# Six of 31 expert blocks added by one-hot products on TensorE, and a weight sum cut into twelve pieces inside the block loop

## The reference, cut to what matters

```
xn = layernorm(x)                                  # layer 1, feed-forward
idx = top_k(xn @ router.T + router_bias, 2)        # 2 of 16 experts a token, no capacity limit
for e in range(16):
    h = silu(xn @ Wu[e]) * (xn @ Wg[e])            # 256 -> 128
    out += combine[:, e:e+1] * (h @ Wd[e])         # 128 -> 256
x = x + tanh(g) * (out + shared_expert(xn))
...                                                # layer 2, attention
gamma_w = clip(mean(abs(w)), 1e-5, None)           # layer 2, feed-forward: for each of 3 weights
w_dq = clip(round(w / gamma_w), -1, 1) * gamma_w   # 256 x 1024 each, ternary
```

## Time and profile before

| what | value |
|---|---|
| median of 3 runs | 891.05 us |
| the profiled execution | 892.17 us |
| its span, first to last instruction | 890.4 us |
| PE, DVE, ACT, POOL busy | 714.0, 534.0, 368.7, 303.3 us |
| mean granted TensorE clock | 0.889 of full speed |
| layer 1's block loop | about 477 to 531 us from the span's start |
| from its end to layer 2's first projection | about 531 to 563 us |

### The profile page before, as it was taken

The page is one execution under the profiler, slowest core; times in us unless marked ns, Lnnn a source line. Parts: engine busy times, 40 slices in busy tenths (PEclk is TensorE's granted clock), DMA queues, the critical chain, the costliest instruction groups (busy, mean ns, idle before and its releaser), DMA issues.

```text
span 890.4 us, 14503 instructions
## 1 busy us (share of the span) xinstructions
PE 714.0 (80%) x5356; PEld 501.8 (56%) x5356; DVE 534.0 (60%) x1244; ACT 368.7 (41%) x658; POOL 303.3 (34%) x332
## 2 busy tenths in 40 slices
PE   5987798997588788887889980892966579999997
PEld 3445465676355555555657860471444446777776
DVE  3896855667899999996475545827776530000014
ACT  4002022424799999996222323342663122221210
POOL 2941130000277777775007506300320072000024
PEclk9997899997899999897898995796898569999999
DMA  7311174520199999999204848000013132515413
GB/s 239 132 59 48 26 148 159 197 74 1 23 176 193 161 198 169 183 174 161 102 25 118 146 126 279 10 0 1 0 54 137 47 87 91 207 48 182 160 39 118
DMA packets 139133, 100.08 MB, mean 112 GB/s; under 512 B 109204, under 2 KB 125238, under 8 KB 137016
## 3 DMA queue, kind: packets, MB, share of 16 engines
q1 hardware_dynamic: 132552, 81.19, 37.8%
q0 software_dynamic: 6224, 17.96, 7.6%
q10 hardware_dynamic: 288, 0.00, 0.0%
HBM read 61.15 MB, written 10.72 MB: 81 GB/s over the span
## 4 chain that ended last, share of the span: by engine, by line
PE 34%; issue 11%; DVE 10%; POOL 4%; ACT 4%; DMA 3%; POOLq 0%; DVEq 0%; ACTq 0%
PE psum L2342 7%; PE psum L2361 5%; PE psum L1661 3%; PE psum L1938 2%; PE psum L214 2%; ACT both L1332 2%; POOL both L568 2%; PE psum L1676 1%; DVE xnT L1438 1%; PE psum L1242 1%; PE psum L2372 1%; PE psum L1520 1%; DMA both<-both 1%; PE psum L621 1%; PE psum L635 1%
## 5 line engine op out<-in xcount | busy, mean ns | idle before, releaser
L1153 POOL TENSOR_SCALAR both<-both 128x1024 f16<-128x1024 f32 x128 | 133.7, 1045 | 162.8 <-ACT both L1332 155.0
L1438 DVE TENSOR_SCALAR_CACHE_REDUCE xnT<-psum,both 128x1024 bf16<-128x1024 f32 x128 | 157.5, 1278 | 9.1 <-PE psum L1242 8.9
L1332 ACT ACTIVATE both<-psum,both 128x1024 f32<-128x1024 f32 x128 | 153.5, 1210 | 9.2 <-DVE xnT L1438 8.7
L1242 PE MATMUL psum<-both 128*128 128x512 bf16 x256 | 84.4, 415 | 32.2 <-ACT both L1332 28.0
L2342 PE MATMUL psum<-both 128*128 128x320 f32 x256 | 73.5, 441 | 3.8 <-ACT both L556 3.8
L1263 PEld LDWEIGHTS psum<-both 128*128 128x128 f16 x1024 | 63.3, 98 | 22.7 <-DMA both<-both 8.3
L2421 ACT ACTIVATE both<-psum 128x320 f32<-128x320 f32 x64 | 27.6, 437 | 110.0 <-PE psum L2342 92.1
L1263 PE MATMUL psum<-both 128*128 128x16 f16 x1024 | 67.7, 171 | 6.4 <-DMA both<-both 2.8
L1264 PE MATMUL psum<-both,minus_base 128*128 128x16 f16 x1024 | 66.5, 170 | 0.0
L1264 PEld LDWEIGHTS psum<-both,minus_base 128*128 128x128 f16 x1024 | 58.6, 98 | 10.8 <-issue 2.7
L2342 PEld LDWEIGHTS psum<-both 128*128 128x128 f32 x256 | 48.8, 194 | 24.1 <-issue 5.3
(11 more groups left out here) (379 smaller groups left out, 1460.5 us busy)
## 6 DMA issues: line engine op xcount, KB each, us to landing
both<-in_l_experts SPq DMA_DIRECT2D x50, 384.0 KB, 3.7
both<-in_l_experts SPq DMA_DIRECT2D x16, 1024.0 KB, 5.5
grouped_y_dram<-both SPq DMA_DIRECT2D x31, 128.0 KB
ctok<-in_ctx SPq DMA_DIRECT2D x2, 1024.0 KB, 7.5
both<-kpad_dram SPq DMA_DIRECT2D x1, 2048.0 KB, 8.0
moe_xn_dram<-xn POOLq DMA_DIRECT2D x4, 512.0 KB, 3.9
both<-bp SPq DMA_DIRECT2D x2, 1024.0 KB, 12.1
moe_y_dram<-both POOLq DMA_DIRECT2D x7, 256.0 KB, 3.1
```

The source lines that it names most:

```text
L1153: nc.gpsimd.tensor_scalar(r2[n % RSLOTS2], e2[:, n % ESLOTS2, :], 255.0, HALF_BASE, ALU.mult, ALU.add).then_inc(sem("r2_ready"), 1)
L1242: last = nc.tensor.matmul(bank[2 * (n % SRING2) + half], qz2[:, h % 2, h // 2, t * P:(t + 1) * P], kT2[:, h // 2, half * 512:(half + 1) * ...
L1332: nc.scalar.activation(e2[:, n % ESLOTS2, :], scores_at(n), ACT.Exp, bias=bias2[:, n:n + 1], scale=s2[:, t * H2 + h:t * H2 + h + 1], accum ...
L1438: nc.vector.tensor_scalar(scaled2[n % 2], scores_at(n), ns2[:, t * H2 + h:t * H2 + h + 1], None, ALU.mult, ALU.min, accum_out=bias2[:, n:n ...
```

## The change

Only blocks 0 to 24 (`STORED3`) are stored and gathered; gathers of pairs in the last six blocks (`OWN3`) get weight 0. For those six, SP writes each token's two slots and weights to device memory, POOL gathers them by lane with six more indirect DMAs, DVE works out a weight for each lane, ACT scales the block's result by it twice (float and bf16), DVE splits it into three bf16 parts, and PE multiplies a one-hot matrix of 128 lanes by 1024 tokens with the parts: 6 blocks x 8 tiles x 3 parts = 144 matmuls, behind the block loop. DVE adds the sums to x from PSUM behind all 16 gathered adds, and only then takes the statistics. The ternary weights are loaded twice: during the block loop one after another into a 1 MB scratch (`wpart5`), where ACT sums quarters of them in iterations 4 to 7, 12 to 15 and 20 to 23, and again at the old place, when all blocks are done. The core of the diff (`part5(j)` issues the 1 MB load of weight j into `wpart5`; `own_add` adds two tiles from a PSUM bank to x; `own_weights` waits for the six lane gathers and takes three small steps):

```diff
+        OWN3 = 6
+        STORED3 = NB3 - OWN3
...
+        OWNS3_AT = (4, 7, 10, 13, 16, 19)
+        PARTS5_AT = (5, 13)
+        WABS5_AT = (4, 12, 20)
...
+            moe0.wait(sp, "weights_ready", 18)
+            shared3.wait(sp, "x_added", 8)
+            sp.dma_start(slot_weight_dram[:, :].rearrange("(t p) k -> p t k", p=P), slot_weight3).then_inc(moe0.sem("weights_ready"), 16)
...
+            part5(0)
+            for b in range(STORED3):
                 block_wait(sp, "y_ready", b + 1)
+                if b in PARTS5_AT:
+                    j = PARTS5_AT.index(b) + 1
+                    sp.wait_ge(sem("wabs_done"), 4 * j)
+                    part5(j)
                 sp.dma_start(moe3.y_dram[b * P:(b + 1) * P, :], y3[:, b, :]).then_inc(moe3.sem("y_stored"), 16)
...
             wsum_tensor(pe)
+            for i in range(OWN3):
+                pe.wait_ge(sem("own_ready"), BLOCKS0 + i + 1)
+                block_wait(pe, "y_ready", STORED3 + i + 1)
+                for t in range(NT):
+                    for k in range(3):
+                        last = nc.tensor.matmul(bank[2 + t // 2][:, t % 2 * D:(t % 2 + 1) * D], own3[i][:, t * P:(t + 1) * P],
+                                                parts3[:, i, k, :], start=(i == 0 and t % 2 == 0 and k == 0),
+                                                stop=(i == OWN3 - 1 and k == 2), skip_group_check=True)
...
+            def own_y(i):
+                b = STORED3 + i
+                block_wait(act, "down_done", b + 1)
...
+                for into in (y3_own[:, i % 2, :], parts3[:, i, 0, :]):
+                    nc.scalar.activation(into, bank[6 + b % 2][:, 0:D], ACT.Copy, scale=own3_weight[:, i:i + 1]).then_inc(sem("own_y"), 1)
...
                 if b + 2 < NB3:
                     copy_rows(b + 2)
-            moe3.wait(act, "y_stored", 16 * NB3)
-            wabs_scalar(act)
+                for j in range(3):
+                    if 0 <= b - WABS5_AT[j] < 4:
+                        wabs_scalar(act, j, b - WABS5_AT[j])
+                if b >= STORED3 + 2:
+                    own_y(b - 2 - STORED3)
...
-            nc.vector.tensor_scalar(idx3[:], kcode3, -1.0, Moe.BIG, ALU.mult, ALU.add).then_inc(moe3.sem("idx_ready"), 1)
-            seq.wait()
+            seq.step(nc.vector.tensor_scalar(kept3, kcode3, Moe.BIG - STORED3 * P, None, ALU.is_gt))
+            nc.vector.tensor_tensor(idx3[:], slot3, kept3, ALU.mult).then_inc(moe3.sem("idx_ready"), 1)
...
+            moe3.wait(dve, "tokens_done", 1)
+            seq.mark(nc.vector.tensor_copy(own3_token, bank[5][:, 384 + STORED3:384 + NB3]))
             moe3.tokens_vector(dve)
...
+            def own(i):
+                nc.vector.tensor_scalar(own3[i], token_row3, own3_token[:, i:i + 1], None, ALU.is_equal).then_inc(sem("own_ready"), 1)
...
+            def own_weights():
+                moe3.wait(dve, "rows0_loaded", 16 * (moe3.groups[0][1] + OWN3))
...
+            def own_parts(i):
+                y, left, parts = y3_own[:, i % 2, :], y3_left[:, i % 2, :], parts3[:, i]
+                dve.wait_ge(sem("own_y"), 2 * BLOCKS0 + 2 * i + 2)
+                seq.step(nc.vector.tensor_tensor(left, y, parts[:, 0, :], ALU.subtract))
+                seq.step(nc.vector.tensor_copy(parts[:, 1, :], left))
+                nc.vector.tensor_tensor(parts[:, 2, :], left, parts[:, 1, :], ALU.subtract).then_inc(sem("block_y_ready"), 1)
...
             for b in range(NB3 + 2):
+                if b in OWNS3_AT:
+                    own(OWNS3_AT.index(b))
+                if b == STORED3 + 1:
+                    own_weights()
...
+                    if m < STORED3:
+                        block_wait(dve, "down_done", m + 1)
+                        nc.vector.tensor_copy(y3[:, m, :], bank[6 + m % 2][:, 0:D]).then_inc(sem("block_y_ready"), 1)
+                    else:
+                        own_parts(m - STORED3)
+
+            gam_vector(dve, seq)
             for n in range(NT * K3):
...
-                if k:
-                    moe3.wait(dve, "added", n + 1)
-                    tile_stats(seq, (t,))
...
+            own_add(0)
+            own_add(1)
+            seq.wait()
+            tile_stats(seq, range(NT // 2))
+            ln_begin(dve, seq, 4, 0)
+            own_add(2)
+            own_add(3)
+            seq.wait()
+            ln_finish(dve, seq, 4, 0)
+            tile_stats(seq, range(NT // 2, NT))
...
             moe3.load_rows_gpsimd(pool)
+            moe0.wait(pool, "weights_ready", 34)
+            moe3.wait(pool, "rows0_loaded", 16 * moe3.groups[0][1])
+            for i in range(OWN3):
+                nc.gpsimd.indirect_dma_start(
+                    out=lane_weight3[:, i, :], out_offset=None, in_=slot_weight_dram[:, :],
...
-            moe3.wait(pool, "y_stored", 16 * NB3)
+            moe3.wait(pool, "y_stored", 16 * STORED3)
```

More of the change, by code:

```diff
@@ L1560, in build @@
         hT3 = r.f32(2, P)
+        kept3 = r.f32(NT, K3)
+        slot_weight3 = r.f32(NT, 2 * K3)
+        lane_weight3 = r.f32(OWN3, 2 * K3)
+        own3_match = r.f32(OWN3, K3)
+        own3_weight = r.f32(OWN3)
+        own3_token = r.f32(OWN3)
+        sh3_at = r.at
+        sh3 = r.f32(2, WN3)
+        assert sh3_at + 2 * HID3 <= W3_AT
+        wpart5 = arena[:, sh3_at:sh3_at + 2 * HID3]
+        y3_own, y3_left = y3[:, STORED3:STORED3 + 2, :], y3[:, STORED3 + 2:STORED3 + 4, :]
+        parts3 = rows3[:, 16:25, :].rearrange("p b d -> p (b d)").bitcast(BF16).rearrange("p (i k d) -> p i k d", i=OWN3, k=3)
+        own3 = [xnT[:, i // 2, i % 2 * 512:(i % 2 + 1) * 512].bitcast(BF16) for i in range(4)]\
+            + [xn[:, 2 * i:2 * i + 2, :].rearrange("p t d -> p (t d)").bitcast(BF16) for i in range(2)]
+        token_row3 = xn[:, 4:8, :].rearrange("p t d -> p (t d)")
+        slot_weight_dram = nc.dram_tensor("slot_weight_dram", [T, 2 * K3], F32)
         idx3 = sb("idx3", [P, NT, K3], I32)
@@ L1692, in l1f_tensor @@
             wsum_tensor(pe)
+            for i in range(OWN3):
[6 more added lines that the diff above has]
+                                                stop=(i == OWN3 - 1 and k == 2), skip_group_check=True)
+                    if i == OWN3 - 1 and t % 2:
+                        last.then_inc(sem("own_done"), 1)
         def l1f_scalar(act):
@@ L1790, in l1f_vector, with own_add @@
                                                ALU.mult, ALU.add).then_inc(moe3.sem("added"), 1)
-                if k:
-                    moe3.wait(dve, "added", n + 1)
-                    tile_stats(seq, (t,))
[L1794 to L1798, removed]
+            moe3.wait(dve, "added", NT * K3)
+            def own_add(b):
+                two = x[:, 2 * b:2 * b + 2, :].rearrange("p a d -> p (a d)")
+                dve.wait_ge(sem("own_done"), OWN_DONE0 + b + 1)
+                seq.mark(nc.vector.tensor_tensor(two, bank[2 + b], two, ALU.add))
+            own_add(0)
[8 more added lines that the diff above has]
+            tile_stats(seq, range(NT // 2, NT))
         def l1f_gpsimd(pool):
             moe3.store_xn_gpsimd(pool)
+            moe3.wait(pool, "xn_stored", 32)
+            pool.wait_ge(sem("xnT_ready"), 4 * turned(3) + 4)
+            nc.gpsimd.iota(token_row3, pattern=[[1, T]], base=1, channel_multiplier=0,
+                           allow_small_or_imprecise_dtypes=True).then_inc(sem("small_consts"), 1)
             moe3.load_rows_gpsimd(pool)
+            moe0.wait(pool, "weights_ready", 34)
[3 more added lines that the diff above has]
+                    out=lane_weight3[:, i, :], out_offset=None, in_=slot_weight_dram[:, :],
+                    in_offset=bass.IndirectOffsetOnAxis(ap=moe3.token_of[:, STORED3 + i:STORED3 + i + 1], axis=0))\
+                    .then_inc(moe3.sem("rows0_loaded"), 16)
             moe3.wait(pool, "idx_ready", 1)
-            moe3.wait(pool, "y_stored", 16 * NB3)
+            moe3.wait(pool, "y_stored", 16 * STORED3)
             for n in range(NT * K3):
@@ L1977, in build @@
         w5 = wring[:, 0:3 * NW].rearrange("p (j n) -> p j n", j=3)
-        wabs5 = sb("wabs5", [P, 3])
+        wabs5 = sb("wabs5", [P, 3, 4])
+        wsum5 = sb("wsum5", [P, 3])
         gam5 = sb("gam5", [P, 3])
@@ L2041, in l2f_sync2, with wabs_scalar @@
                              A[name].rearrange("(c p) n -> p c n", p=P)).then_inc(sem(f"ring_loaded{4 + j}"), 16)
[L2043 to L2048, removed]
+        def wabs_scalar(act, j, i):
+            act.wait_ge(sem(f"ring_loaded{4 + j}"), RING0_LOADS + 16)
+            some = wpart5[:, i * NW // 4:(i + 1) * NW // 4]
+            nc.scalar.activation(some, some, ACT.Abs, accum_out=wabs5[:, j, i:i + 1]).then_inc(sem("wabs_done"), 1)
         def wsum_tensor(pe):
-            pe.wait_ge(sem("wabs_done"), 3)
+            pe.wait_ge(sem("wabs_done"), 12)
             pe.wait_ge(sem("small_consts"), 6)
             block_wait(pe, "h_ready", NB3)
```

(5 more changed lines are left out.)

46 lines of the change are left out of this document (33 added, 13 removed).

## The result

After, the median is 904.7 us (904.0 to 907.0, four executions), beside 890.9 before: 13.8 us slower, a ratio of 1.0151 with a 95% interval of 1.0119 to 1.0184. The forecast was 894.4 us in a range of 889.0 to 900.5: the direction was right, the size was not. The profiled execution took 905.3 us.

The account below looks back on a forecast made before the run. PE bounds the block loop; behind it the y gathers, issued by POOL, and DVE's layer norm. Ahead +0.3, load waits +2.0, gathers -3.7 and tail +4.8 sum to +3.4: 891.05 becomes 894.4 us, range 889.0 to 900.5.

Parts of the forecast that it names:

- Waits put into the loop: Block loop: ACT waits for three 1 MB loads, with PE soon needing what follows; +2.0 us, bounds 0 and 6.
- Third load: Block loop, about 505.5 to 513 us: ACT waits 0.5 to 4 us for it, taken 1.7.
- First load: Start of the block loop: issued about 479, wanted about 486.7; first two loads given 0 to 1.5 us wait, taken 0.3.
- rival B: Block loop: third load or lane gathers 4 us or more late, PE's clock falls; +9, 900 us; chance 0.17.
- Ahead of the loop: Before the block loop: two more dependent steps of 0.17 us before the token list PE waits for; +0.3 us.
- ACT's quarters and DVE's builds: Block loop: quarter sums and one-hot builds fit into idle time of ACT and DVE; free, 13.5 us without that cover.
- Gathers: Behind the loop: first and sixteenth y gathers issued 7.7 us earlier; 3.7 of this left after slower landing.
- The last landing: Sixteenth y gather: takes 6.7 us instead of 2.7 because the loads are moving, landing at 551.0.
- DVE's tail: Behind the last gather: adds, statistics and layer norm no longer under gathers; from 5.8 to 10.6 us, +4.8.
- Rival A: Block loop: no load is late, so only 1.4 us is left; 892.5 us; chance 0.22.
- Rival C: Sixteenth y gather: lands in 2.7 us although loads move, tail starts 4 us earlier; -2.6, 888.4 us; chance 0.13.

Follow-up runs that it names:

- e12: Changed kernel with one number changed: the third load's quarters summed at blocks 26 to 29 in place of 20 to 23; 896.4 us.
- e1: Changed kernel with the three loads and twelve quarter sums taken out of the block loop, whole sums back behind the y stores; one-hot blocks stay; 891.4 us.
- e9: Changed kernel with the three loads and their quarters at later places, the first load after the second group of row gathers has landed; 897.9 us.
- e4: Changed kernel with empty lanes reading the row of their own lane number, not all row 0; 895.7 us.
- e7: Changed kernel with spread lanes, earlier first load, second weight loads and masks held until the last y gather landed, query, key, value weights loaded in the loop; 891.5 us.

## Why the prediction was wrong in size

By medians the 13.8 us fall apart into 904.7 - 896.4 = 8.3 for the second stall (e12 takes it alone away), 896.4 - 891.4 = 5.0 for what e12 still has over e1, and 0.5 for the one-hot part. In the profiles these 5.0 lie ahead of block 3 (22.5 and 17.4), so they are the first stall; a part of them may be the store's (e9).

- **The failing step is "Waits put into the loop", +2.0 with bounds 0 and 6.** It measured about 13 (8.3 + 5.0). *Third load:* the time that it may take, 7.4 us, was right (14.79 - 7.38 = 7.4). Its own time was priced by ctok's 8.2 us, raised to at most 7.4 + 4, though the trace showed the engines 0.99 busy at 108 GB/s where it falls and row gathers at 8.7. Nor was little else moving beside ctok: two loads of 384 KB went out ahead of it on SP's queue, and from 423 to 425 us the engines were 0.98 busy at 372 GB/s. There were no gathers there. I saw the place and took the price from another. *First load:* I asked only whether ACT would wait for it; ACT didn't. That the load slows the row gathers issued beside it, which PE needs sooner, had no term; I looked at this only for the last row group. With the half clock behind both stalls, which only rival B priced, the bound of 6 was too low.
- **Rival B** (0.17, 900 us) named the mechanism of the second stall, a third load 4 us or more late and PE at half clock behind it. Its +9 held 1.4 and some 7.6 for that stall, which measured 8.3; what it lacked is the first stall.
- **Ahead of the loop, +0.3:** the first row gather came at 466.59, not later than before; too small to tell.
- **ACT's quarters and DVE's builds at nothing:** right. A quarter and its read take 0.72 us from start to end, and the loop's pace in e1, e4 and e12 is that of before.
- **Gathers, -7.7:** right, -8.1 in e1. **The last landing, 6.7 us:** right, 6.30, and for the reason given, as e7 shows. **DVE's tail, 10.6:** right, 575.60 - 565.3 = 10.3. Together -3.7 + 4.8 was +1.1, and e1's second half of xn is 0.5 later.
- **Rival A** (1.4 without late loads, 892.5): its condition failed, but its sum is near what e1 measured without the loads, 891.4.
- **Rival C** failed: the last gather took 6.30.
- Of the 15.1 us by which the second half of xn is later (575.60 against 560.46), 1.0 comes back at once: the projections behind it take 14.55 us in place of 15.60 in the chain. The span's end is 12.3 later. At the last layer norm (692.1 us before) the delay is still 14.8, so the rest comes back behind it; how is not traced.

By the Trainium skill (DMA: Bandwidth & Descriptors, "Queues, rings and completion order") each DMA engine takes turns between the queues that have work for it, a packet at a time. In the second stall the trace agrees: from 512 to 525 us SP's queue moved 1996 packets and POOL's 273. In the first it doesn't show it: from 480 to 483 us SP's queue moved 96 packets and POOL's none, though its gather of 477.96 landed only at 485.9; the cause of this stays open. The same page's fit, from which the prediction's estimate of 4.4 us for 1 MB was worked out ("Anatomy of one DMA — SWDGE (gpsimd) path"), is for GpSimd's DMAs; here SP's loads took 5.9 us in e4 and 14.8 in the changed kernel, so it is no price for a load beside gathers.

## What to carry to other kernels

Ahead of putting a load under a loop, price its landing time from transfers in the very stretch where it will run, and ask whether the gathers that the loop needs next can bear it. A high DMA share at a low rate (here 0.99 at 108 GB/s) is a warning: a load put there took 14.8 us, and 5.9 once the lanes were spread. Padding indices that all point at one row can cause it: give them different rows, or move the waiting use away, which here took one number.

## What was not expected of the hardware

Here gathers that read one row again and again were slow with no load beside them. From the two rows above, a packet of POOL's queue held an engine for 0.659 x 16 x 19 us / 524 = 0.38 us with the empty lanes on row 0, and 0.342 x 16 x 19 / 597 = 0.17 us with the lanes on different rows, at the same mean of 2.7 KB a packet. What in the memory's path makes it so, these runs don't show.
